# Feed-forward stage of a Perceiver block: first products five tiles ahead, four tiles in flight, and the last stores of a stage awaited one stage later

## What is computed

```python
x = x + xattn(layernorm(x), ctx, w_q, w_k, w_v, w_o, b_o)
x = x + attn(layernorm(x), w_attn, w_proj, decay_raw)
# feed-forward: q rounds to multiples of 2**-8, gelu is linear between
# 33 points on [-4, 4] (step 0.25), 0 below, identity above
h = q(layernorm(x) @ w1 + b1)          # 2048 rows x 2048
h = q(pwlin_gelu(h))
x = x + q(h @ w2 + b2)                 # 2048 rows x 512
```

## Time and profile before

| | |
|---|---|
| median of 3 runs | 1655.59 us (1654.24 to 1659.61) |
| the profiled execution | 1653.21 us, its span 1651.2 us |
| TensorE busy | 1587.2 us, 96% of the span |
| VectorE busy | 1251.0 us, 76% |
| ScalarE busy | 1031.5 us, 62% |
| GpSimd busy | 781.5 us, 47% |
| self attention begins | 999.0 us into the span |
| feed-forward begins | 1260.2 us |
| its last down product ends | 1644.9 us |

### The profile page before, as it was taken

The page is one execution under the profiler, slowest core; times in us unless marked ns, Lnnn a source line. Parts: engine busy times, 40 slices in busy tenths (PEclk is TensorE's granted clock), DMA queues, the critical chain, the costliest instruction groups (busy, mean ns, idle before and its releaser), DMA issues. The chain is left out here.

```text
span 1651.2 us, 30240 instructions
## 1 busy us (share of the span) xinstructions
PE 1587.2 (96%) x11126; PEld 1384.3 (84%) x11126; DVE 1251.0 (76%) x2396; ACT 1031.5 (62%) x2050; POOL 781.5 (47%) x730
## 2 busy tenths in 40 slices
PE   6999999999999999999999999999987999999997
PEld 4888899998999989899998788889876777878786
DVE  5548888877887888788786874666665989888887
ACT  3338777777777777677786423444445666666665
POOL 3116546464564546455462331334444655555553
PEclk9999999999999999999999999999988999999999
DMA  9773434444343443534452952012132121010010
GB/s 268 219 241 100 124 108 107 125 110 133 89 127 109 107 128 103 135 102 110 118 138 83 306 194 59 32 47 78 66 103 82 53 70 58 13 58 20 20 39 26
DMA packets 173827, 173.64 MB, mean 105 GB/s; under 512 B 80944, under 2 KB 138352, under 8 KB 173680
## 3 DMA queue, kind: packets, MB, share of 16 engines
q1 hardware_dynamic: 173680, 171.71, 35.7%
HBM read 133.91 MB, written 37.75 MB: 104 GB/s over the span
## 5 line engine op out<-in xcount | busy, mean ns | idle before, releaser
L75 PE MATMUL p_bank_score<-p_ctxt,p_qo 128*128 128x256 f32 x2304 | 304.6, 286 | 1.0 <-ACT p_probs L999 0.7
L75 PEld LDWEIGHTS p_bank_score<-p_ctxt,p_qo 128*128 128x128 f32 x2304 | 288.1, 191 | 6.1 <-issue 2.4
L75 PE MATMUL p_bank_mix<-p_probt,p_ctx 128*128 128x512 f32 x1152 | 292.1, 398 | 0.5
L75 PEld LDWEIGHTS p_bank_mix<-p_probt,p_ctx 128*128 128x128 f32 x1152 | 207.6, 189 | 41.7 <-issue 3.7
L1980 PE MATMUL p_bank_down<-p_w,p_ht 128*128 128x512 f32 x768 | 190.4, 397 | 14.2 <-DVE p_ht L2078 10.8
L1196 DVE SCALAR_TENSOR_TENSOR p_qo<-p_bank_mix,p_odd,p_qo 128x512 fp32r<-128x512 f32 x192 | 143.8, 749 | 57.4 <-ACT p_qo L1013 49.7
L1980 PEld LDWEIGHTS p_bank_down<-p_w,p_ht 128*128 128x128 f32 x768 | 143.3, 189 | 50.3 <-issue 12.4
L1951 POOL TENSOR_TENSOR p_a<-p_a,p_g 128x512 f32<-128x512 f32 x64 | 108.0, 1688 | 160.4 <-ACT p_a L2025 160.4
L705 POOL TENSOR_TENSOR p_ctx<-p_ctx_in,p_ctx 128x768 fp32r<-128x768 f32 x64 | 118.2, 1847 | 131.7 <-ACT p_ctx L988 131.4
L1013 ACT ACTIVATE p_qo<-p_bank_mix,p_odd 128x512 fp32r<-128x512 f32 x192 | 132.3, 689 | 68.0 <-PE p_bank_mix L75 67.6
L999 ACT ACTIVATE p_probs<-p_bank_score,p_small 128x257 f32<-128x257 f32 x256 | 121.3, 475 | 58.9 <-DVE p_small L1177 55.1
(11 more groups left out here) (277 smaller groups left out, 3668.1 us busy)
## 6 DMA issues: line engine op xcount, KB each, us to landing
p_blocks_in<-in_ctx_dram SPq DMA_DIRECT2D x256, 96.0 KB, 2.4
p_ctx_in<-in_ctx_dram SPq DMA_DIRECT2D x64, 384.0 KB, 3.1
q<-p_ctx SPq DMA_DIRECT2D x64, 256.0 KB, 3.2
p_odd_in<-in_ctx_dram SPq DMA_DIRECT2D x64, 192.0 KB, 3.5
p_x<-in_x_dram SPq DMA_DIRECT2D x32, 256.0 KB, 4.1
p_quad<-q SPq DMA_DIRECT2D x32, 256.0 KB, 3.7
p_probt<-q SPq DMA_DIRECT2D x32, 256.0 KB, 4.4
p_o_in<-o SPq DMA_DIRECT2D x8, 1024.0 KB, 6.9
```

The costliest lines, as they stand in the source:

```text
L75: made = e.matmul(out, lhsT, rhs, start=n == 0, stop=n == last)
```

## The change

1. `SETS` is 4 and `LAG` is 5. `ht` has four buffers. The GELU pieces `a` (high place) and `g0` (low place) of a tile lie in the same memory as the two halves of `ht` of that tile. So Abs of tile n waits for the down products of tile n-4 (`downed`), and the other two waits on ScalarE for used buffers go.
2. The steps of the next group's rows are two passes apart, not three, with `LOADED`, `SCALED`, `TURNED`, `SPLIT` = 5, 6, 7, 8. TensorE turns a tile after the down product of its pass. The two halves of the turned rows are written a pass later, early in it: on ScalarE ahead of Abs, on VectorE right behind the low half of tile n-2.
3. The end of a group is handled in one portion, in passes 20, 36, 52 and 68: ScalarE's four roundings ahead of Abs, VectorE's four sums and four outputs ahead of the snap. SyncE stores four tiles in a row.
4. SyncE no longer waits at the end of the first two parts. It waits for those stores (`x1_gone`, `x2_gone`) in the next part: ahead of the first three loads into the y tiles (whose ring now lies first in memory), and at pass 2 of the feed-forward part.

```diff
     SETS = 4          # was 3
     LAG = 5           # was 3
...
+        with ExitStack() as second:
+            pieces = [second.enter_context(nc.sbuf_tensor(f"p5_pieces{i}", [P, 2, G], F32)) for i in range(SETS)]
+        ht = room.ring("ht", SETS, [P, 2, G], F32R)
+        a_, g0_ = ([pair[:, i, :] for pair in pieces] for i in range(2))
...
-        LOADED, SCALED, TURNED = 3, 4, 5
+        LOADED, SCALED, TURNED, SPLIT = 5, 6, 7, 8
...
                 if n < NT:
                     up(n)
-                    for i in tile_at(n, TURNED):
-                        norm.turn(e, i)
                 if n >= LAG:
                     down(n - LAG)
+                for i in tile_at(n, TURNED):
+                    norm.turn(e, i)
...
+                for i in tile_at(n, SPLIT):
+                    norm.high(e, i, zts[(g + 1) % 2], i % NR * P)
+                for done in done_at(n):
+                    for i in range(NR):
+                        rounded_sum(done * NR + i)
                 if n < NT:
                     e.wait_ge(rounded, n + 1)
                     if n >= SETS:
-                        e.wait_ge(summed, n - SETS + 1)
+                        e.wait_ge(downed, NR * (n - SETS + 1))
                     e.activation(a[:], m[:], ACT.Abs, bias=minus[:]).then_inc(absed, 1)
...
                 if 1 <= n <= NT:
-                    if n >= 3:
-                        e.wait_ge(downed, NR * (n - 2))
                     e.wait_ge(fixed, n)
...
+                for i in tile_at(n, SPLIT):
+                    norm.low(e, i, zts[(g + 1) % 2], i % NR * P)
                 for done in done_at(n):
-                    for i in range(2):
-                        down_sum(done * NR + i)
-                for done in done_at(n - 1):
-                    for i in range(2, NR):
-                        output(done * NR + i)
+                    for i in range(NR + 2):
+                        if i >= 2:
+                            output(done * NR + i - 2)
+                        if i < NR:
+                            down_sum(done * NR + i)
...
-            for i in range(3):
-                e.wait_ge(y_out[i], DMA * len(range(i, NT, 3)))
...
+                if n == 2:
+                    for i in range(3):
+                        e.wait_ge(x2_gone[i], DMA * len(range(i, NG * NR, 3)))
```

More of the change, by code:

```diff
@@ L1342, in cross_attention, with self_attention @@
             block.sync(sync)
-        return wattn, wproj, ahead, room.used
-def self_attention(nc, ahead, after, x1_dram, wattn, wproj, decay_raw, w_1, x2_dram, x2_moments, ended):
+        return wattn, wproj, ahead, x1_gone, [s for s in room.used if s not in x1_gone]
+def self_attention(nc, ahead, after, x1_dram, x1_gone, wattn, wproj, decay_raw, w_1, x2_dram, x2_moments, ended):
     G = ahead.group
@@ L1459, in sync @@
             for i in range(3):
+                e.wait_ge(x1_gone[i], DMA * len(range(i, NT, 3)))
+            for i in range(3):
                 load_y(i)
@@ L1815, in feed_forward @@
     KT, KF = C // P, F // P
-    SETS = 3
-    LAG = 3
+    SETS = 4
+    LAG = 5
     MAGIC = 1.5 * 2.0 ** 15
@@ L1868, in tile_at @@
             g, f = divmod(n, KF)
-            return [(g + 1) * NR + (f - first) // 3] if n < NT and g + 1 < NG and f >= first and (
-                f - first) % 3 == 0 and (f - first) // 3 < NR else []
-        LOADED, SCALED, TURNED = 3, 4, 5
+            return [(g + 1) * NR + (f - first) // 2] if n < NT and g + 1 < NG and f >= first and (
+                f - first) % 2 == 0 and (f - first) // 2 < NR else []
+        LOADED, SCALED, TURNED, SPLIT = 5, 6, 7, 8
         def done_at(n):
@@ L2028, in scalar @@
                             high_block(k)
[L2029 to L2031 removed]
                 if 1 <= n <= NT:
[L2033 to L2034 removed]
                     e.wait_ge(fixed, n)
[L2036 removed]
+                    e.activation(ht[(n - 1) % SETS][:, HI, :], m_[(n - 1) % SETS][:], ACT.Identity,
                                  bias=minus[:]).then_inc(h_hi, 1)
@@ L2095, in vector @@
                                            op1=ALU.subtract).then_inc(apart, 1)
-                    for i in tile_at(n, TURNED):
-                        norm.low(e, i, zts[(g + 1) % 2], i % NR * P)
                     if n == 1:
                         low_block(0)
-                for done in done_at(n):
-                    for i in range(2):
-                        output(done * NR + i)
-                        down_sum(done * NR + i + 2)
-                    if n == NT + LAG - 1:
-                        for i in range(2, NR):
-                            output(done * NR + i)
                 if 0 <= n - 1 < NT:
@@ L2144, in build @@
         with ExitStack() as weights:
-            wattn, wproj, ahead, ended = cross_attention(
+            wattn, wproj, ahead, x1_gone, ended = cross_attention(
                 nc, kept, weights, ident, ident_ready, x_rows, L0_xattn_w_q, L0_xattn_w_k, L0_xattn_w_v, L0_xattn_w_o, L0_xattn_b_o,
```

34 lines of the change are left out of this document (9 added, 25 removed).

## The result

| | before | after |
|---|---|---|
| median of 4 runs | 1655.82 us (1654.24 to 1659.61) | 1683.84 us (1682.7 to 1684.2) |
| ratio to before, 95% interval | 1 | 1.0165 [1.0147, 1.0183] |
| profiled execution (span) | 1653.21 us (1651.2) | 1684.08 us (1682.0) |
| first up to end of last down, in that span | 384.6 us | 417.0 us |
| mean granted clock of TensorE | 0.992 | 0.986 |

The change makes the kernel 28.0 us slower on the medians. Two executions stood apart and enter no ratio: one of e8 took 8812 us (without it the median of e8 is 1658.61 and not 1658.93), and one of the kernel before, beside e1 to e4, took 1752 us at a granted clock of 0.847.

The account below looks back on a forecast made before the run. It took TensorE's product time as the bound, with VectorE also near its limit in group 0. 2.7 + 9.6 + 12.3 + 2.4 + 1.2 - 2.2 = +26.0 us, giving 1682 us, range 1667 to 1695.

Parts of the forecast that it names:

- group 0: First 512 rows of the feed-forward stage: VectorE sets the pace, then the turn loop; +2.7 us.
- D(21): Time when TensorE has finished pass 21 of its loop, up(21) and down(21-LAG); forecast at 1394.1 us.
- borders: Ends of the two stages ahead of feed-forward: SyncE no longer waits for last stores, 1.1 us each, -2.2 us.
- eight turns: Transpositions of rows in groups 1 and 2: each waits 1.6 us for scaled rows, +12.3 us.
- second and third change of group: TensorE waits for emptied down banks, losing 5.3 us each; before they lost 1.0 together: +9.6 us.
- the clock: TensorE's clock falls after its rest at each group change, 0.8 us each (0 to 1.7): +2.4 us.
- tail: From the end of the last up to the end of the last down, 20.3 us: +1.2 us.
- What was left to win: TensorE's removable waits in the feed-forward stage: about 9 us in group 0, 3.5 behind it.
- rival (a): TensorE stays fed if the chain from finished down to scaled rows is under 5.57 us: 1641 us, chance 7%.
- The new wait: ScalarE's Abs of tile n waits for down(n-4), some 8 us after its input is ready, making VectorE late.
- Rival (c): VectorE collides more with GpSimd: one microsecond per turn and 0.68 for six low halves, 1694 us, chance 15%.
- (b): Turns are hidden and only group changes cost: 1669 us, chance 13%.

Follow-up runs that it names:

- e8: Kernel before with lag four, four tiles in flight, the shared place and last stores awaited a stage later, old order of steps: 1658.93 us, ratio 1.0013.
- e1: Changed kernel with own two buffers for the GELU pieces, lag five kept, second bias left out to make room: 1651.93 us, ratio 0.9973.
- e4: Changed kernel with a group's sums, roundings and outputs one pass earlier on VectorE and ScalarE: 1679.01 us, ratio 1.0146.
- e2: Changed kernel with a lag of four instead of five, shared place kept: 1650.92 us, ratio 0.9973.
- e7: Kernel before with only the last stores of the first two parts awaited one part later: 1653.87 us, ratio 0.9980.
- e5: Changed kernel with rows loaded and scaled, and halves of turned rows written, one pass earlier: 1668.26 us, ratio 1.0061.
- e9: e2 with GpSimd splitting all but the first block of the second weights: 1648.20 us, ratio 0.9949.
- e11: e9 with e5's edit (scaling and halves of turned rows a pass earlier): 1650.92 us, ratio 0.9967.

## Why the prediction was right, step by step

Predicted were 1682 us by +26.0 on the profiled execution; measured are 1683.84 and +30.8. The mechanism is shown by e1 and e2, and the sum was close. That the median is only 2 us off is in part luck: on the two profiled executions the sum is 4.8 us short, and half of that goes because the one of before lies 2.6 us under its median. On the two profiled spans:

| step | predicted | measured |
|---|---|---|
| group 0 up to D(21), borders within it | +1.3 | +4.3 |
| eight turns | +12.3 | +11.6 |
| second and third change of group, with the clock | +11.2 | +10.6 |
| up(32) and up(48) waiting for turned rows | not seen | +1.6 |
| tail | +1.2 | +1.4 |
| not placed | | +1.3 |

The first row predicted is 2.7 for group 0, 0.8 for the clock, less 2.2 for the borders; measured is 1395.62 against 1391.37. The last is what is left of 30.8.

**What was left to win** was read too low. The prediction has about 9 us in group 0, the 8.8 for low halves. With the 3.2 us of turns and 2.4 us at the first change of group TensorE rested 14.4 us between its first four products and 1392 us. The forecast itself does not hang on it, since it goes by when products are done; the 1641 of rival (a) does.

**The new wait.** Right: Abs waits in 54 tiles, for down(n-4).

**Turns.** Right. The eight waits are 12.1 us (four of 1.58, four of 1.44 to 1.48), less the 0.5 of before. The low half of turned rows ahead of a scaling did cost nothing, as argued. VectorE's timeline ahead of the turn at 1524.98:

```profile
1523.52 0.68 DVE L164 TENSOR_TENSOR p_zt<-p_bank_turn,p_zt 128x512 fp32r<-128x512 f32 x1
1524.12 0.80 DVE L142 TENSOR_SCALAR p_x<-p_x,p5a_ln_minus,p5a_ln_inv 128x512 f32<-128x512 f32 x1
```

The scaling takes 0.80 us instead of 1.39, because it starts 0.6 us later behind the low half. It ends 0.3 us after GpSimd's multiplication, which ended at 1524.64, as it did before (1501.70 after 1501.41). At the first turn of group 1, where no low half stands ahead of it, it takes 1.38 us, and the turn waits as long as the three behind it, 1.58 us. So the scaling waits for GpSimd and the waits do not add up. With this the trace agrees with what the prediction cites from the Trainium skill (Perfetto Trace Analysis, Optimizing Scalar/DVE Operations), that GpSimd and VectorE share a port that is held under an exclusive lock. Rival (c), which adds these times up at the turns, is false here.

**Group changes and clock.** The rests were 3.66, 3.57 and 3.66 us (3.7 predicted), and D(20) to D(21) took 11.2, 10.9 and 11.8 us (10.9 predicted without the clock). The clock fell all three times; busy times and clock (third from the end) just behind the three rests:

```profile
1390.90:1395.60 4.70, 4.63 (x12) 3.00 (x13) 4.11 (x7) 2.72 (x4) 0.32 (x1) 0.64 0.30 112
1494.50:1499.00 4.50, 4.41 (x13) 3.35 (x14) 3.90 (x7) 2.77 (x4) 0.36 (x1) 0.66 0.31 117
1598.20:1603.50 5.30, 5.26 (x13) 4.13 (x14) 4.46 (x7) 2.71 (x4) 0.30 (x1) 0.51 0.33 121
```

The level is a mixture of 1.2 and 2.4 GHz, but it cost 0.3, 0.0 and 0.9 us where 0.8 each was taken. The down at 1390.95 takes 4.84 us instead of 2.9, but most of that would have gone into waiting for its last bank. The term was 1.2 too large.

**Group 0** is the step of the sum that was off most: 3.0 us. D(8) was 3.5 late against the predicted 1307.0 (1309.2 less the borders), D(14) 4.1, D(20) 3.4. So the miss lies ahead of D(8); the loop behind it was right (13.25 us for two passes, 13.0 predicted). TensorE's timeline there:

```profile
1282.80 4.50 PE L75 MATMUL p_bank_up<-p5a_zt,p_wattn 128*128 128x512 f32 x12 [2.49 <-DVE p_m L2067]
...
1302.70 1.11 PE L153 MATMUL p_bank_turn<-ident,p_x 128*128 128x128 f32 x4 [7.07 <-DVE p_x L142]
1303.46 4.41 PE L75 MATMUL p_bank_up<-p5a_zt,p_wattn 128*128 128x512 f32 x12
...
1310.48 2.98 PE L75 MATMUL p_bank_up<-p5a_zt,p_wattn 128*128 128x512 f32 x12
```

TensorE had run ahead and then rested 7.07 us before the first turn. Behind the rest the granted clock was 0.62 from 1302.7 to 1307.7: the turn took 0.76 us to the next start instead of 0.41, and the up took 4.41 instead of 2.98, together 1.8 us. The prediction counted that rest as harmless stock used up, and counted no fall of the clock for it.

VectorE began tile 6 at 1299.6 where 1298.0 was expected (1300.2 less the borders): 1.6 us. Of these, 0.6 lie ahead of the part, whose first product began at 1258.66 and not at 1258.05 (1260.25 less 2.2). The other 1.0 fits the scaling, which the prediction took off at its full 1.39 us, though it takes 0.53 where nothing holds it up. Counted from the first product, VectorE reached tile 6 only 1.1 us sooner than before, not 2.1. Three other operations now met GpSimd, which worked from 1289.34 to 1293.96 with gaps of 0.3 us at most: L2090, L2098 and L2101 took 1.67, 1.79 and 1.54 us from 1289.56 on, where each takes 0.7 elsewhere. A wait for GpSimd that is taken from one operation can come back at the next; the prediction argued just this for the turns and not here.

**What was not seen:** up(16), up(32) and up(48) wait 0.75, 0.89 and 0.75 us for the last low half of turned rows (L164). It is the same chain: that half is written in the same late VectorE pass. The prediction listed what TensorE wants from early in a pass and left this one out, though the diff moves it there.

**Tail.** The last down ended 20.5 us behind the end of the last up (20.3 predicted): 1655.19 to 1672.65+3.02.

```profile
1655.19 8.32 PE L1982 MATMUL p_bank_down<-p_w,p_ht 128*128 128x512 f32 x36
1672.65 3.02 PE L1982 MATMUL p_bank_down<-p_w,p_ht 128*128 128x512 f32 x12 [0.90 <-DVE p_ht L2072]
```

**Stage ends.** VectorE's idle time in front of the next stage is 0.33 and 0.32 us, before 1.54 and 1.53: 2.4 us off against 2.2 predicted, and e7 gives 2.6. In the profiled execution the feed-forward part began only 1.6 us sooner, because cross attention, ahead of both borders, ended 0.7 us later in it.

**The rivals.** (a), TensorE stays fed, named its own condition, a chain shorter than a pass. It was not met; where an experiment met it (e1, e2), the time was 1651 to 1652, not 1641, because TensorE's waits of 14.7 and 15.8 us in all stay, nearly all of them in group 0 and at its end. (b), turns hidden, is what e5 builds: 1668.3 against the 1669 worked out for it, which is in part luck, since e5 also freed the up products and its first rest grew by 4.0 us.

## What to carry to other kernels

When one buffer serves two roles, write down in which pass of the consumer it comes free: a producer at tile n that waits for the consumer of tile n-S runs (LAG-S) passes behind, so S must be at least LAG, or the lag is paid for in lateness. Such lateness costs nothing until an engine demands something with less than a pass of slack; list every such demand (rows, bank, last half), since repairing one sends the wait to the next, and only the repair of all shows what it was worth (15.6 and 4.8 us alone, 31.3 together). What a longer lag and a shared place cost depends on the order of the steps around them, too: a lag of four with the shared place cost 5 us in the old order (e7 to e8), and e2, in the new one, is 7 us below e8.

## What was not expected of the hardware

**The order of steps decides which operations collide.** The last addition of a tile from 1400 to 1640 us, in the view of one line (count, shortest/median/longest in ns), before and after:

```profile
L2114 DVE SCALAR_TENSOR_TENSOR p_m<-p_m,p_g x44: 691/693/1673, 1401.7 to 1639.5; 128x512 f32<-128x512 f32 x44
```

```profile
L2101 DVE SCALAR_TENSOR_TENSOR p_m<-p_m,p_pieces x38: 691/692/694, 1404.5 to 1639.6; 128x512 f32<-128x512 f32 x38
```

Before, eight of the 44 took 1.66 to 1.67 us, at the eight tiles in whose pass the low half of turned rows (L164) stands ahead of the last two operations. After, not one of 38 is longer than 694 ns. It would be natural to say that the new wait does it, because Abs ties both engines to TensorE's pace. Two runs speak against that. In e1 Abs waits for no down product, and in e8 it waits as in e2 but in the old order of steps:

```profile
L2099 DVE SCALAR_TENSOR_TENSOR p_m<-p_m,p_g x44: 691/692/694, 1403.2 to 1637.1; 128x512 f32<-128x512 f32 x44
```

```profile
L2112 DVE SCALAR_TENSOR_TENSOR p_m<-p_m,p_pieces x42: 691/693/1667, 1404.7 to 1638.2; 128x512 f32<-128x512 f32 x42
```

So the long ones go with the order in which the half of the turned rows stands, and not with the wait. Over the whole part this operation's busy time falls from 57.5 to 46.1 us, about half of the 24 us by which VectorE is less busy; a slower kernel can have the cleaner operations.

**How long a rest lowers the clock** is not the same each time. Rests of 3.57 to 3.66 and of 7.07 us were followed by low clock; so were one of only 2.49 us, at 1282.80, whose up took 4.50 us, and the one of 2.22 us ahead of the part's first product at 1258.66 (0.64 granted over the next 4.8 us). The rest of 3.21 us in the earlier trace rows was not. None of the rests of 1.4 to 1.9 us was. The same rest can go either way: after 2.64 us ahead of a down product the granted clock was 1.00 in e9 and 0.62 in e11. What decides between them is not shown.
